# The sine half of the queries' rotary: four ACT copies of 32 partitions in place of two PE products, in an attention block between two mixtures of experts

## The reference, cut to what matters

```
q = rms_norm(hidden @ wq_a, q_a_norm_w) @ wq_b        # 16 heads x (64 plain + 64 rotary)
q_nope, q_pe = q[..., :64], q[..., 64:]
q_pe = q_pe * cos + rotate_half(q_pe) * sin           # rotate_half: [-second 32, first 32]
attn = softmax(([q_nope, q_pe] @ [k_nope, k_pe].T) * 128 ** -0.5)
out = (attn @ v) @ wo
```

## Time and profile before

| | |
|---|---|
| median of 3 runs | 1088.32 us (1087.28 to 1092.0) |
| the profiled execution's own time | 1089.1 us |
| its span, first to last instruction | 1087.3 us |
| granted TensorE clock, mean | 0.979 |
| busy share of PE, DVE, ACT, POOL | 93%, 68%, 48%, 44% |
| PE busy from 660 to 720 us (attention) | 60.00 of 60.00 us |
| ACT busy there | 41.31 us |
| DVE busy there | 47.40 us |

### The profile page before, as it was taken

One profiled execution on the slowest core, in us unless ns is written; L12 is line 12 of the kernel. 1 busy time (PEld: TensorE's weight loads), 2 busy tenths in 40 slices (PEclk: granted clock), 3 DMA queues, 4 the chain that ended last, 5 costly groups with the idle time before them and its releaser, 6 DMA issues.

```text
span 1087.3 us, 22878 instructions
## 1 busy us (share of the span) xinstructions
PE 1015.2 (93%) x6183; PEld 803.4 (74%) x6184; DVE 734.1 (68%) x1677; ACT 518.0 (48%) x1133; POOL 477.7 (44%) x418
## 2 busy tenths in 40 slices
PE   5569999999889999999999999999999889999995
PEld 4448888887558777777778777777788558888884
DVE  7725666745577788877887788788556845766642
ACT  2213334422366676767767677777411214443421
POOL 3723443433343644645463644443125514443422
PEclk9979999999899999999999999999999989999998
DMA  9836455431101101111011110111567545544330
GB/s 330 217 112 158 103 114 136 81 49 26 58 1 49 40 22 40 40 40 40 21 40 40 40 39 23 39 40 40 182 216 241 178 117 116 160 109 110 48 58 7
DMA packets 72098, 95.66 MB, mean 88 GB/s; under 512 B 9840, under 2 KB 49008, under 8 KB 71984
## 3 DMA queue, kind: packets, MB, share of 16 engines
q1 hardware_dynamic: 56560, 76.76, 22.4%
q0 software_dynamic: 14304, 16.87, 9.2%
q10 hardware_dynamic: 1152, 1.06, 0.4%
HBM read 64.14 MB, written 34.43 MB: 91 GB/s over the span
## 4 chain that ended last, share of the span: by engine, by line
PE 86%; DVE 8%; issue 2%; ACT 1%; DMA 1%; POOL 1%; POOLq 0%; SPq 0%; DVEq 0%; ACTq 0%
PE bank L1759 11%; PE bank L1786 11%; PE bank L1576 7%; PE bank L1574 7%; PE bank L1578 7%; PE bank L1747 5%; PE bank L1749 5%; PE bank L1748 5%; PE bank L1859 4%; PE bank L1586 4%; PE bank L1588 3%; PE bank L1587 3%; PE bank L1559 3%; PE bank L1734 2%; PE bank L1735 2%
## 5 line engine op out<-in xcount | busy, mean ns | idle before, releaser
L918 ACT ACTIVATE shared<-bank,small 128x512 f32<-128x512 f32 x256 | 176.5, 690 | 90.9 <-DVE small L1387 89.9
L1387 DVE TENSOR_REDUCE small<-bank 128x1 f32<-128x512 f32 x256 | 174.5, 684 | 41.7 <-PE bank L1749 41.6
L835 ACT CAST split_rows_and_inner<-bank 128x512 fp32r<-128x512 f32 x78 | 45.8, 587 | 237.8 <-PE bank L1559 237.8
L1759 PE MATMUL bank<-constants,shared 128*128 128x128 f32 x1024 | 156.3, 275 | 2.3 <-ACT shared L918 0.7
L1759 PEld LDWEIGHTS bank<-constants,shared 128*128 128x128 f32 x1024 | 122.3, 141 | 44.9 <-issue 13.9
L1576 PE MATMUL bank<-expert_weights_low,split_rows_and_inner 128*128 x312 | 144.3, 463 | 0.0
L1578 PE MATMUL bank<-expert_weights_high,split_rows_and_inner 128*128 x312 | 143.4, 460 | 0.0
L1574 PE MATMUL bank<-expert_weights_high,split_rows_and_inner 128*128 x312 | 125.4, 402 | 2.5 <-DVE split_rows_and_inner L1166 2.5
L1747 PE MATMUL bank<-expert_weights_high,shared_split 128*128 128x512 f32 x256 | 122.5, 479 | 2.4 <-POOL shared_split L662 1.4
L653 POOL TENSOR_TENSOR shared<-shared 128x512 f32<-128x512 f32 x32 | 41.2, 1289 | 188.9 <-DVE shared L1397 185.5
L1171 DVE TENSOR_TENSOR split_rows_and_inner<-bank,split_rows_and_inner 128x512 fp32r<-128x512 f32 x78 | 53.9, 692 | 103.9 <-ACT split_rows_and_inner L835 103.9
(11 more groups left out here) (201 smaller groups left out, 2190.1 us busy)
## 6 DMA issues: line engine op xcount, KB each, us to landing
expert_weights<-w SPq DMA_DIRECT2D x32, 512.0 KB, 4.5
shared<-rows_by_expert SPq DMA_DIRECT2D x78, 129.0 KB, 2.1
expert_weights<-wo SPq DMA_DIRECT2D x16, 512.0 KB, 6.8
shared<-inverse_sums SPq DMA_DIRECT2D x64, 128.0 KB, 2.9
attended_transposed<-shared SPq DMA_DIRECT2D x32, 256.0 KB, 3.1
expert_weights<-attended_transposed SPq DMA_DIRECT2D x2, 2048.0 KB, 10.0
shared<-attended_transposed SPq DMA_DIRECT2D x2, 2048.0 KB, 10.4
expert_weights_low_plain<-x_after_moe SPq DMA_DIRECT2D x4, 512.0 KB, 9.0
```

What stands on the lines that cost most here:

```text
L918: nc.scalar.activation(prob[k % 4], bank[k % 4][:, :], ACT.Exp, bias=negmax[:, k % 8:k % 8 + 1], accum_out=psum[par][:, hh * GT + qt:hh * ...
L1387: V.tensor_reduce(negmax[:, k % 8:k % 8 + 1], bank[k % 4][:, :], AX.X, ALU.max, negate=True).then_inc(max_ready, 1)
L1759: last = tr(bank[4 + k % 2][:, c * P:(c + 1) * P], prob[k % 4][:, c * P:(c + 1) * P], ident)
```

## The change

From the third pair on (p >= 2) part 1 is no longer made on PE. ACT copies the rotary rows from bank 7 into `ropeB`, by quarters of 32 partitions and crosswise (quarter 0 from quarter 1 and the reverse, 2 from 3 and the reverse). The sign moves into the table of sines. DVE then multiplies `ropeB` in place by the sines, in step 0 of the next pair.

- ACT gets `queries_turned(p + 2)` in step 4 of pair p (step 5 of the first pair): a wait for `ropeA_sb`, a wait for `rope_ready`, and four copies of 32 x 512.
- PE loses `queries(p + 2, par, 1)` behind step 6. Its part 2 now waits for `turned_sb`.
- DVE's `ropes(p, 1)` moves from step 7 to step 0, with both inputs in SBUF.
- POOL splits two of the three parts of the weights from the third pair on.
- The second set of weights is written for the first two pairs alone.

```diff
-    c[:, C_SIN:C_ALL] = np.tile(sin.T, (4, 1))
+    c[:, C_SIN:C_ALL] = np.concatenate([-sin.T, sin.T, -sin.T, sin.T])
...
             def load_weights(p, par):
-                src = wpair[:, p % PAIRS, :, :]
+                parts_ = slice(0, 3) if among(p, 0, 1) else slice(0, 3, 2)
+                src = wpair[:, p % PAIRS, parts_, :]
...
+            def queries_turned(p):
+                act.wait_ge(ropeA_sb, p + 1)
+                act.wait_ge(rope_ready, p)
+                for a in range(4):
+                    b = a + 1 - 2 * (a % 2)
+                    last = nc.scalar.copy(ropeB[a * HALF:(a + 1) * HALF], bank[7][b * HALF:(b + 1) * HALF, :])
+                last.then_inc(turned_sb, 1)
...
+                    if k == (5 if first else 4) and p + 2 < NPAIR:
+                        queries_turned(p + 2)
                     if k in BY_ACT:
                         copy_pT(p, par, k)
...
-                    last = V.tensor_scalar(wpair[:, :, 1, at + (1 - two) * HALF:at + (2 - two) * HALF], src[:, :, hh, :],
-                                           norm_w[:, 0:1], -1.0 if two else 1.0, ALU.mult, ALU.mult)
+                    last = V.tensor_scalar(wpair[:, 0:2, 1, at + (1 - two) * HALF:at + (2 - two) * HALF], src[:, 0:2, hh, :],
+                                           norm_w[:, 0:1], None, ALU.mult)
...
-                    dve.wait_ge(qb_psum, p + 1)
-                    V.tensor_tensor(ropeB, query_bank(p, 1)[:, :], qsin, ALU.mult).then_inc(ropeB_sb, 1)
+                    if among(p, 0, 1):
+                        dve.wait_ge(qb_psum, p + 1)
+                        turned = query_bank(p, 1)[:, :]
+                    else:
+                        dve.wait_ge(turned_sb, p - 1)
+                        turned = ropeB
+                    V.tensor_tensor(ropeB, turned, qsin, ALU.mult).then_inc(ropeB_sb, 1)
...
-                    if k == 7 and not among(p, NPAIR - 2, NPAIR - 1):
-                        ropes(p + 2, 1)
+                    if k == 0 and not first and not last:
+                        ropes(p + 1, 1)
...
+                elif among(p, 1):
+                    pe.wait_ge((ropeA_sb, ropeB_sb)[part - 1], p + 1)
                 elif not among(p, 0):
-                    pe.wait_ge((ropeA_sb, ropeB_sb)[part - 1], p + 1)
+                    pe.wait_ge(turned_sb, p - 1)
...
-                    if k == 6 and p + 2 < NPAIR:
-                        queries(p + 2, par, 1)
```

More of the change, by code:

```diff
@@ L338, in build @@
         qa_psum, qb_psum, qz_psum = sem("qa_psum"), sem("qb_psum"), sem("qz_psum")
+        turned_sb = sem("queries_turned")
         ropeA_sb, ropeB_sb, rope_ready = sem("ropeA_sb"), sem("ropeB_sb"), sem("rope_ready")
@@ L638, in load_weights @@
             def load_weights(p, par):
-                src = wpair[:, p % PAIRS, :, :]
+                parts_ = slice(0, 3) if among(p, 0, 1) else slice(0, 3, 2)
+                src = wpair[:, p % PAIRS, parts_, :]
                 if p > 1:
                     pool.wait_ge(qz_psum, p - 1)
-                nc.gpsimd.tensor_copy(wch[par], src).then_inc(wc_high, 1)
+                nc.gpsimd.tensor_copy(wch[par][:, parts_, :], src).then_inc(wc_high, 1)
                 pool.wait_ge(wc_high, p + 1)
                 pool.sem_inc(pool_issue, 1)
-                nc.gpsimd.tensor_tensor(wcl[par], src, wch[par].bitcast(F32), ALU.subtract).then_inc(wcur_ready, 1)
+                nc.gpsimd.tensor_tensor(wcl[par][:, parts_, :], src, wch[par][:, parts_, :].bitcast(F32),
+                                        ALU.subtract).then_inc(wcur_ready, 1)
             def rope_sum(p):
```

## The result

The changed kernel takes 1105.9 us (median of 4 runs, 1105.17 to 1107.26) against 1089.49 us in 4 runs of the kernel before (1087.28 to 1092.0). The ratio is 1.0158, 95% interval 1.0137 to 1.0179. The forecast was 1106 us. The profiled execution took 1107.26 us with a span of 1105.4 us.

A forecast was written before the change was run, and what follows sets the result against it. PE, 93% busy with 86% of the chain, was taken as bound, but made late by ACT's copies. Pair losses of 18.5 us, the 14.1 saved already out, plus 1089.1 gave 1107.6; less 0.8, 1106.8, rounded to 1106; range 1091 to 1112 us.

The forecast's parts named there:

- The saving, 0.47 us a pair: On PE ahead of tile 7's transposes: two products removed, 0.47 us in each of 30 pairs, 14.1 us if nothing comes late.
- The length of a copy: On ACT: a copy of 32 x 512 takes 0.58 us, as one of 128 x 512, so quartering saves nothing.
- The pitch and the block: On ACT between tile 6's and tile 7's exponentials: four copies without overlap, 0.61 us each, 2.44 us together.
- the 0.03 us of start: On ACT: 0.03 us from the end of the read of tile 6's sum to the first copy, without overlap.
- The rival of overlapping copies: On ACT: copies overlap by 0.10 us, 4 x 0.48 = 1.92 us; +4 us, 1092 us in all; chance 0.15.
- 0.4 for pair 0: Estimated loss of 0.4 us in pair 0, at a lower rate of work.
- The way to PE: From tile 7's exponential: its transposes 0.84 us later, step 0 2.08 us later; PE idles 1.16 us ahead of those transposes.
- The classes of pairs: Step 0's lateness: plain 0.80 us, j = 6 1.02, j = 1, 5 0.51, j = 0, 3, 7 0.75; j = 2 gains 0.40.
- What was to cost nothing: DVE's moved sine product, POOL's later sum and shorter splits, PE's part 2 wait, L1270 about 1 us smaller: no cost.
- the rival of a loss passed on: POOL's sum and its high part on ACT come late, ACT waits in step 1: 15 us more, 1121 us; chance 0.07.
- The bound of 0.5 us for a product from SBUF: DVE's sine product with both inputs in SBUF takes between 0.5 us and POOL's 1.29 us.
- The faster rival: Four copies under 1.28 us fit ACT's hole ahead of tile 7's exponential; 14.1 us gained in full, 1074 us; chance 0.08.

The follow-up runs named there:

- the run with copies and products: The kernel before plus the change's four ACT copies, with part 1's two products kept on PE: 1105.01 us, ratio 1.0157.
- straight quarters: The changed kernel with each quarter copied from the same partitions it goes to, without the exchange of halves: 1102.04 us in a single execution.
- one copy: The changed kernel with one straight copy of 128 x 512 in place of the four crosswise copies: 1081.12 us, ratio 0.9942.
- copies by columns: The changed kernel with its four copies cut by columns, 128 x 128 each, without the exchange of halves: 1081.4 us, ratio 0.9935.
- two groups alone: The changed kernel with quarters 0 and 1 copied where they were, 2 and 3 in step 7 behind tile 9's exponential: 1101.5 us, ratio 1.0127.
- with part 2 moved as well: Against the kernel of two groups alone, PE's part 2 moved from step 0 to step 1, ahead of `attend`: 1084.12 us, ratio 0.9952.
- another order: The changed kernel with its quarters copied in the order 1, 2, 3, 0: 1103.66 us in a single execution.

## Why the prediction was right

**The total, and the luck in it.** The time came out within 0.1 us of 1106, and that closeness is luck. The prediction adds 18.5 us to one kernel before of 1089.1 us and then rounds down by 0.8; the difference measured is 16.4 us, and the kernel before, taken along with the change, had a median of 1089.49 us where the prediction started from 1088.32. What was right is the mechanism: which engine is late, at which step, and by how much in each class of pairs.

**The saving, 0.47 us a pair.** Read rightly as PE's time, and rightly not credited: the run with copies and products showed that it is worth nothing while tile 7's exponential is late.

**The length of a copy.** 0.58 us was forecast for 32 x 512 from the durations of 128 x 512 and 8 x 128; it measured 0.578. Those two rows differ in columns and in partitions, so they don't by themselves show that partitions cost nothing; the 0.58 of L933 on 64 partitions was the better support.

**The pitch and the block.** 0.61 a copy and 2.44 us to the next exponential were forecast; from 706.75 to 709.12 it is 2.37. The reading that no overlap comes about where the start partition changes holds in every kernel with quarters here, but the prediction took it by the partition written, and that is only half of it. The first of the four copies writes partition 0, as the read of the sum ahead of it does; by the prediction's own rule it should have overlapped, and it didn't, since it reads partition 32 (with straight quarters it reads 0 and overlaps by 0.10). So the 0.03 us of start was right without its reason. The rival of overlapping copies fell with the pitch of 0.59. The 0.07 us by which I was too high, times the 26 pairs in which ACT is last, is 1.8 us; the 18.5 us that I summed, less 0.4 for pair 0, which ended before the first of the transposes counted, is 1.2 us above the 16.9 measured. The 0.4 for pair 0 isn't shown by any trace: ACT idled 0.47 us for DVE behind that pair's copies, so they were not last there, and from the transposes of tile 0 to the first inverse transpose it took 22.76 us after and 24.47 before, in a stretch (296 to 340 us) where the granted clock was 1.00 after and 0.94 before.

**The way to PE.** Tile 7's transposes 0.84 us behind its exponential: 0.83 (709.12 to 709.95). Step 0 2.08 us behind it: 2.07 (to 711.19). PE idle ahead of tile 7, forecast 1.16: the row says 0.90, and by the pitch of PE (0.23 us from L1769's start at 708.65) it is 1.07.

**The classes of pairs.** The table above. The pair j = 2, the only one to gain, and j = 6, the one that lost most, came out within 0.02 us. j = 0, 3 and 7 were 0.06 to 0.10 too high, about the 0.07 of the block. The same 0.07 should have shown in the others; the plain pairs and j = 4, 5 and 6 came out 0.02 to 0.08 below the forecast, but j = 1 0.03 above it. What fills the difference stays open, but for the 0.04 us named below.

**What was to cost nothing.** DVE's product from SBUF takes 0.683 us, as from a bank (0.680), and POOL's sum starts at 712.81, while ACT takes it from 714.78 without a wait: the rival of a loss passed on didn't happen. From step 0 of the plain pair to the next inverse transpose it is 7.62 us before (697.07 to 704.69) and 7.66 after (711.19 to 718.85): the loss is not given back there and grows by 0.04. The bound of 0.5 us for a product from SBUF stood in no row; the sum didn't use it. L1270 got smaller by some 0.4 us (four times 0.34 before, 0.25 after) and not by 1, without effect on anything.

**The faster rival** needed four copies in 1.28 us. No kernel here had a mean pitch under 0.58 between copies of quarters. Its price of 14.1 us was wrong as well: the kernels with one copy and with copies by columns meet its condition and gain 5.1 us in the pairs, since behind them it is DVE's maximum of tile 8, its exponential and the copy of tile 6 that come last. The prediction doesn't have that chain; it made no difference to the forecast, since ACT was late by more.

## What to carry to other kernels

An engine at half load can still be the one that comes last at a given step: look for the idle time just ahead of the next instruction whose result the bound engine waits for, and compare the moved block with that, not with the engine's share. An ACT copy cost by its columns here and not by its partitions (0.578 us for 32 x 512, 0.580 for 128 x 512, 0.283 for 128 x 128), so cutting a tile into quarters by partitions made four copies of full price out of one. When work has to go onto such an engine, split it so that each part stands in a stretch where the engine has time, and move the consumers of the moved work later with it: two groups alone took 1101.50 us, with part 2 moved as well 1084.12.

## What the runs showed of the hardware that I had not expected

In these kernels ACT instructions overlap the one before by 0.10 to 0.12 us only where both the partition read and the partition written start as those of the instruction before; the prediction had only the partition written. Copies of quarters have a mean pitch of 0.58 to 0.59 us at a length of 0.58 us, those cut by columns 0.16 us at a length of 0.28 us. Read and write partition were told apart in the first copy of each block alone, in three kernels (the change, straight quarters, another order).
